# A graph kernel on one core: keys as int16 pairs for the left one-hot comparison, node numbers of the relational products in a PSUM bank, h2 transposed by fours

## The chip, the cores and the metric

One core of a Trainium2 chip runs the whole kernel as one program. The metric is the device time of an execution in microseconds (us). The engines are PE (matmuls), DVE (VectorE), ACT (ScalarE), POOL (GpSimd) and SP (which issues DMAs). SBUF is the on-chip memory; PSUM has 8 banks of 512 floats per partition.

## The reference

Two graph layers with residuals on 3125 nodes of 128 features and 50000 edges, sorted by destination, with 64 edge types. The first propagates three times over the normalized adjacency; the second is relational, with 64 relation matrices combined out of 16 bases.

```python
# layer 0
h = relu(layernorm(x));  cur = acc = h @ W_in + b_in
deg = segment_sum(1, src);  w = deg^-1/2[src] * deg^-1/2[dst]
for _ in range(3):
    cur = segment_sum(cur[dst] * w, src);  acc += cur
x = x + (acc / 4) @ W_out + b_out
# layer 1
h = relu(layernorm(x));  W_rel = einsum('rb,bio->rio', w_comp, weight)
agg = segment_sum((h @ W_rel[type])[src] * norm, dst)
x = x + relu(agg + h_bias + h @ loop_weight)
```

## The kernel before, in words

The 50000 edges lie in 391 tiles of 128, one edge per partition. The 3125 destinations are cut into 200 windows of 16 nodes, eight windows to a group of 128 nodes, 25 groups. Since the edges are sorted by destination, a step through tiles and windows has 391 + 200 - 1 = 590 pairs (tile, window). They are worked in 59 turns of U = 10 pairs.

**Setup** (to about 45 us). DVE and PE work out, for all 590 pairs at once, the destination within the window (`dlP`), the high part of the source with it (`keyP`, L649: destination times 8 plus source block) and the low part of the source (`loP`). They stand one column per pair in SBUF, as floats.

**Counting stage** (to about 345 us). It builds the dense matrix of edge counts, bf16, 128 rows per group. For each pair DVE makes two one-hot matrices over the 128 edges: the left one (128 columns, `ohA`) for five pairs in one instruction of 640 elements (L751), by comparing the numbers 0 to 127 with the pair's key, and the right one (400 columns, `ohB`, L754), one instruction per pair. There are three buffers of five pairs each. PE multiplies the two (L992) into the PSUM bank of the window; six banks go round. ACT takes two finished windows at a time out of PSUM (L1215) and clears the banks (L1217), SP writes them to their rows by DMA (L426). In turns 0 to 48, DVE, PE and POOL also make the 16 coefficients of each edge out of its type (L721, L727, L735, L1000, L518, L529); from turn 49 on PE adds the degrees in between (L1017).

**Propagation** (to about 528 us): PE's products of the dense matrix with the features (L1067), with small DVE steps between blocks, then layer norm of the result, stored to HBM as h2.

**Relational stage** (from 531 us to the end). It goes through the pairs in reverse order, from the last window to the first. POOL gathers, for each of the 391 tiles, the 128 rows of h2 of its sources from HBM by an indirect DMA whose indices lie in SBUF (L563) into a ring of 64 places (GRING); from the 65th on it waits, once for every four gathers (GSTEP), that the pairs of the tile that had the place are made. SP counts landed gathers in order for DVE. For each pair DVE copies the tile's rows next to each other (L873, 128 floats) and makes the other operand (L876, `scalar_tensor_tensor`, 256 elements): for each of 16 bases and 16 nodes of the window, coefficient if the edge's destination is that node, else zero. It compares `iota16` (int16 in SBUF) with a scalar per partition of `dlP` and multiplies by the coefficient (SBUF, float). PE multiplies (L1135, fp32, two records a pair) into one of four banks by window; ten pairs are buffered. ACT copies each closed window out (L1276) and clears its bank (L1279); after eight windows PE makes the group's output (L1115, L1116), ACT adds the bias (L1284). At the start PE transposes h2 (L1102, 25 tiles of 128) in five batches of five over two pairs of banks, 4-5 and 6-7, and ACT copies them out (L1263, 640 columns). Ahead of the last turn and behind it, outputs are transposed back into banks 6 and 7 (L1158) and added to x2 (L891).

Order: each engine's program is written out by hand; the waits on semaphores set the rest. The loop of DVE for the relational stage is a run of `operands(c)` for turns 1 to 57, then parts of `add_x2`, then turn 58.

```python
for u in range(U):                       # operands(c), L863
    if u % 2 == 0:
        dve.wait_ge(gathered, counts[u + 1][1])      # L868
        if not first:
            dve.wait_ge(pairs2, c * U + (u + 2 - U)) # L870
```

Of the kernel before, what the change touches and what calls it, by code (L numbers as in the profile page):

```python
# [34 lines left out]
I16 = mybir.dt.int16  # L35
U16 = mybir.dt.uint16
ALU = mybir.AluOpType
# [4 lines left out]
P = 128  # L42
# [4 lines left out]
BASES = 16  # L47
# [4 lines left out]
NG = -(-N // P)  # L52
# [4 lines left out]
WIN = 16  # L57
# [3 lines left out]
HI = P // WIN  # L61
LO = NPAD // HI
S = NT + NW - 1
U = 10
TURNS = S // U
HALF = S // 2
RING = 4
CRING = 6
COEF_BANK = 6
SIXTH, SIXTH_SHIFT = 10923, 16  # L70
# [10 lines left out]
HU = U // 2  # L81
# [3 lines left out]
BATCH = 5  # L85
# [6 lines left out]
H_TURNS = -(-NG // 4)  # L92
# [63 lines left out]
def build(nc, x, src, dst, etype, norm, W_in, b_in, W_out, b_out, weight, w_comp, h_bias, loop_w, out):  # L156
    assert TURNS * U == S
    ctx = ExitStack()
    with ctx:
# [15 lines left out]
        acc = sb("acc", [P, NG, HID], F32)  # L175
        stage = sb("stage", [P, WPG, LO], BF16)
        keys = sb("keys", [P, 2 * S], F32)
        keyP, loP = keys[:, 0:S], keys[:, S:2 * S]
        tab_count = sb("tab_count", [1, TURNS, len(GROUPS)], I32)
        dlP = sb("dlP", [P, S], F32)  # L180
        src_col = sb("src_col", [P, NT], I32)
        iota16 = sb("iota16", [P, LO], I16)
        ident = sb("ident", [P, P], F32)
# [27 lines left out]
        ohA = [h[:, 0:HU * P].rearrange("p (u k) -> p u k", u=HU) for h in halves]  # L211
# [6 lines left out]
        ps = ctx.enter_context(nc.psum_tensor("ps", [P, 8, 512], F32))  # L218
        psf = ps[:, :, :].rearrange("p b n -> p (b n)")
# [4 lines left out]
        at = [0]  # L224
# [14 lines left out]
        at = [0]  # L239
# [68 lines left out]
        h2T = carve2(NPAD)  # L308
# [271 lines left out]
        def _(dve):  # L580
            count = [0]

            def step(ins, wait=True):

                count[0] += 1
                ins.then_inc(dve_c, 1)
                if wait:
                    dve.wait_ge(dve_c, count[0])
# [57 lines left out]
            pairs_of = lambda b: ps[:, b:b + 2, 0:HALF]  # L646
            split = lambda row: row.rearrange("p (h s) -> p h s", h=2)
            step(dve.scalar_tensor_tensor(split(dlP[:]), split(ws_s[:]), float(-WIN), pairs_of(0), ALU.mult, ALU.add))
            step(dve.scalar_tensor_tensor(split(keyP), split(dlP[:]), float(HI), pairs_of(2), ALU.mult, ALU.add), False)  # L649
            step(dve.tensor_copy(split(loP), pairs_of(4)), False)  # L650
            step(dve.tensor_copy(src_col[:], ps[:, 6, 0:NT]), False)
            step(dve.tensor_copy(norm_col[:], ps[:, 7, 0:NT + 1]), False)
# [87 lines left out]
            def onehots(c, phase, loaded=None, stored=None, coefs=True):  # L740


                for u in range(U):
                    h = (2 * phase + u // HU) % HALVES
                    s = c * U + u
                    col = slice(s, s + 1) if isinstance(s, int) else ds(s, 1)
                    if u % HU == 0:
                        if not isinstance(s, int) or s >= HALVES * HU:
                            dve.wait_ge(pairs_done, c * U + (u - (HALVES - 1) * HU))
                        cols = slice(s, s + HU) if isinstance(s, int) else ds(s, HU)  # L750
                        dve.tensor_tensor(ohA[h][:], iota16[:, 0:P].unsqueeze(1).broadcast_to([P, HU, P]),  # L751
                                          keyP[:, cols].unsqueeze(2).broadcast_to([P, HU, P]),
                                          ALU.is_equal).then_inc(oh_ready, 1)
                    dve.tensor_scalar(ohB[h][:, u % HU, :], iota16[:], loP[:, col], None, ALU.is_equal).then_inc(oh_ready, 1)  # L754
                    if u == COEF_TYPES and loaded is not None:
                        type_rows(c, phase, loaded)
                    if u == COEF_SUM and coefs:
                        sum_parts(c - 1)
                    if u == COEF_OUT and coefs:
                        finish_coefs(c - 1, (phase - 1) % HALVES, stored)  # L760
# [91 lines left out]
            between_blocks(NB - 1)  # L852


            dve.wait_ge(ld_coef, 16)
            pairs = Turn(dve, "pair", NT)
            iota_w = iota16[:, 0:WIN].unsqueeze(1).broadcast_to([P, BASES, WIN])

            def operands(c, first=False):
                row = slice(TURNS - 1 - c, TURNS - c) if isinstance(c, int) else ds(c * -1 + (TURNS - 1), 1)  # L860
                dve.load(pairs.new_word(), tab_pair[0:1, row])
                counts = [pairs.first()]
                for u in range(U):  # L863
                    if u % 2 == 0:
# [4 lines left out]
                        if not first:  # L869
# [3 lines left out]
                    dve.tensor_copy(gpair[:, u:u + 1, :], gring[:, ds(pairs.place(total, GRING), 1), :]).then_inc(pair_in, 1)  # L873
                    dl = dlP[:, back:S - U + back + 1]
                    dl = dl[:, S - U - c * U:S - U - c * U + 1] if isinstance(c, int) else dl[:, ds(c * -U + (S - U), 1)]
                    dve.scalar_tensor_tensor(kpair[:, u, :, :], iota_w, dl,  # L876
                                             coef_flat[:, ds(tiles * -BASES + NT * BASES, BASES)].unsqueeze(2)
                                             .broadcast_to([P, BASES, WIN]),
                                             ALU.is_equal, ALU.mult).then_inc(pair_in, 1)
# [15 lines left out]
            dve.wait_ge(x2_in, 16)  # L895
            for i in range(len(OUT_PARTS) - 1):
                add_x2(i)
            operands(TURNS - 1)
            add_x2(len(OUT_PARTS) - 1)


# [1 line left out]
        def _(pe):  # L903
# [190 lines left out]
            for r in range(RING):  # L1094
                pe.matmul(ps[:, r, :], zb, zw, start=True, stop=True).then_inc(slots2, 1)
            pe.wait_ge(h2_in, 16)
            for b in range(NG // BATCH):
                if b >= 2:
                    pe.wait_ge(h2_copied, b - 1)
                for i in range(BATCH):  # L1100
                    at = 2048 + (b % 2) * 1024 + i * P
                    last = pe.transpose(psf[:, at:at + P], h2[:, b * BATCH + i, :], ident[:])  # L1102
                last.then_inc(h2_turned, 1)
            pe.wait_ge(h2_copied, NG // BATCH)
            pe.wait_ge(ld_two, 48)

            def group_output(g):
# [70 lines left out]
        def _(act):  # L1178
# [78 lines left out]
                    make_h2(b - 1)  # L1257
            make_h2(NB - 1)

            for b in range(NG // BATCH):  # L1260
                act.wait_ge(h2_turned, b + 1)
                at = 2048 + (b % 2) * 1024
                act.copy(h2T[:, b * BATCH * P:(b + 1) * BATCH * P], psf[:, at:at + BATCH * P]).then_inc(h2_copied, 1)  # L1263

            act.sem_inc(routed, 2)

# [66 lines left out]
```

## Time and profile before

| | before |
|---|---|
| median of 3 runs | 1063.05 us (1062.24 to 1063.17) |
| the profiled execution, its own time | 1060.07 us |
| its span | 1058.5 us |
| PE busy | 835.4 us (79%) |
| DVE busy | 777.0 us (73%) |
| POOL busy | 477.5 us (45%) |
| ACT busy | 357.5 us (34%) |
| mean granted TensorE clock | 0.886 of 2.4 GHz |

How to read it: busy times are sums of instructions over the whole span, so an engine that bounds one stage and rests in another shows a middling share. A duration is from an instruction's start to its end; consecutive instructions of DVE overlap by somewhat under 0.1 us, so that spacing is the better measure of cost. Releasers of waits are inferred. The spacing of POOL's instructions includes the time for issuing.

### The profile page before, as it was taken

Reading aid. Unit: us, or ns where it says so; the run is one execution under the profiler, and the core shown is the slowest. Engines: PE = TensorE matmul, PEld = TensorE weight load, DVE = VectorE, ACT = ScalarE, POOL = GpSimd, SP = SyncE. Lnnn points to the kernel's source line nnn. Section 1 sums busy time; section 2 is a strip of 40 time slices with the busy share of each in tenths; the row PEclk is TensorE's granted clock in tenths of the full one; section 3 lists DMA queues with packets and bytes.
Section 4 is the critical chain, followed back from the end, with each engine's and each line's share of the span. In section 5 each row is a group of like instructions: output and inputs, shape, how many; then the busy total and the mean of one; then the engine's idle time right before and its main releaser. Section 6 shows DMA issues by size and latency. Waiting matters only on the chain.

```text
span 1058.5 us, 27160 instructions
## 1 busy us (share of the span) xinstructions
PE 835.4 (79%) x5567; PEld 594.8 (56%) x5571; DVE 777.0 (73%) x2436; ACT 357.5 (34%) x706; POOL 477.5 (45%) x532
## 2 busy tenths in 40 slices
PE   4667667677698699999719889988888988888676
PEld 2622222222255699999517667666665665565345
DVE  7879999999984645434617777787778788888554
ACT  0402355677777000001315444443434332221000
POOL 2022323333200000010167777777777777777773
PEclk9687886977866899999858999999999999999868
DMA  4012334455534000011591111111112112111113
GB/s 114 1 45 67 85 103 107 125 131 128 132 101 107 2 1 2 1 32 51 146 298 49 48 50 50 50 50 47 52 47 52 50 50 52 50 52 51 51 50 89
DMA packets 64847, 73.24 MB, mean 69 GB/s; under 512 B 12803, under 2 KB 53178, under 8 KB 64666
## 3 DMA queue, kind: packets, MB, share of 16 engines
q1 hardware_dynamic: 48362, 37.30, 12.7%
q0 software_dynamic: 16432, 35.29, 12.6%
q8 instruction: 26, 0.43, 0.2%
q14 instruction: 27, 0.22, 0.1%
HBM read 43.85 MB, written 8.22 MB: 49 GB/s over the span
## 4 chain that ended last, share of the span: by engine, by line
PE 35%; DVE 26%; issue 15%; DVEq 9%; DMA 7%; POOL 5%; ACT 1%; SPq 1%; POOLq 0%; ACTq 0%
PE ps L1067 14%; PE ps L1135 10%; DMA CT<-h_dram,src_col 6%; POOL CT L563 5%; DVE ohbuf L754 5%; DVE CT L873 5%; PE ps L992 4%; PE ps L1115 3%; DVE u L754 3%; DVEq L876 3%; DVE CT L876 3%; DVE ohbuf L751 3%; DVEq L122 2%; DVEq L873 2%; DVE u L751 1%
## 5 line engine op out<-in xcount | busy, mean ns | idle before, releaser
L563 POOL DMA_INDIRECT CT<-h_dram,src_col x391 | 393.9, 1007 | 125.1 <-issue 95.4
L1135 PE MATMUL ps<-CT 128*128 128x256 f32 x1180 | 316.9, 418 | 71.7 <-DVE CT L876 46.3
L1135 PEld LDWEIGHTS ps<-CT 128*128 128x128 f32 x1180 | 211.3, 198 | 171.7 <-issue 151.9
L876 DVE SCALAR_TENSOR_TENSOR CT<-iota,dlP,CT 128x256 f32<-128x256 int16 x590 | 286.8, 486 | 5.6
L873 DVE COPY CT<-CT 128x128 f32 x590 | 137.7, 233 | 139.2 <-PE ps L1135 72.6
L1276 ACT COPY CT<-ps 128x256 f32<-128x256 f32 x200 | 77.7, 388 | 328.5 <-PE ps L1135 324.6
L992 PE MATMUL ps<-ohbuf 128*128 128x400 bf16 x395 | 126.6, 422 | 48.2 <-DVE ohbuf L754 34.6
L518 POOL DMA_DIRECT2D u<-types_dram x49 | 44.0, 904 | 198.8 <-PE ps L1000 185.1
L1215 ACT CAST stage<-ps 128x800 bf16<-128x800 f32 x100 | 82.4, 824 | 123.1 <-PE ps L992 122.8
L1067 PE MATMUL ps<-u,CT 128*128 128x192 bf16 x1250 | 107.4, 248 | 6.9 <-DVEq L804 6.9
L1067 PEld LDWEIGHTS ps<-u,CT 128*128 128x128 bf16 x1250 | 104.3, 99 | 9.0 <-DVEq L804 8.3
L992 PEld LDWEIGHTS ps<-ohbuf 128*128 128x128 bf16 x395 | 40.4, 102 | 122.6 <-issue 98.4
L754 DVE TENSOR_SCALAR ohbuf<-iota,keys 128x400 bf16<-128x400 int16 x395 | 102.4, 319 | 0.0
L1115 PE MATMUL ps<-CT 128*128 x800 | 95.8, 277 | 7.0 <-ACT CT L1276 4.8
L1115 PEld LDWEIGHTS ps<-CT 128*128 128x128 f32 x800 | 91.2, 191 | 16.9 <-issue 16.9
L992 PE MATMUL ps<-u 128*128 128x400 bf16 x195 | 64.3, 432 | 29.3 <-DVE u L754 17.2
L1217 ACT COPY ps<-zeros 128x800 f32<-128x800 f32 x100 | 83.0, 830 | 8.7
L551 POOL TENSOR_TENSOR ohbuf<-ohbuf,keys 128x640 f32<-128x640 f32 (+2 forms) x6 | 7.8, 1310 | 155.6 <-DMA ohbuf<-x 155.6
L1279 ACT COPY ps<-zeros 128x256 f32<-128x256 f32 x200 | 75.2, 376 | 6.5
L751 DVE TENSOR_TENSOR ohbuf<-iota,keys 128x640 bf16<-128x640 int16 x79 | 64.7, 819 | 9.5 <-PE ps L992 6.5
L1236 ACT ACTIVATE keys<-ps 128x256 f32<-128x256 f32 (+1 forms) x6 | 2.2, 366 | 161.5 <-PE ps L1041 161.5
L837 DVE COPY stage<-ps 128x320 f32<-128x320 f32 (+2 forms) x18 | 7.9, 436 | 66.2 <-PE ps L1067 65.7
(171 smaller groups left out, 653.9 us busy)
## 6 DMA issues: line engine op xcount, KB each, us to landing
CT<-stage SPq DMA_DIRECT2D x200, 100.0 KB, 3.0
u<-types_dram POOLq DMA_DIRECT2D x49, 128.0 KB, 3.5
CT<-h_dram,src_col POOLq DMA_INDIRECT x391, 2.6
coef_dram<-coef_out POOLq DMA_DIRECT2D x49, 64.0 KB, 3.4
CT<-coef_dram SPq DMA_DIRECT2D x1, 3048.0 KB, 11.9
out<-CT SPq DMA_DIRECT2D x4, 256.0 KB
ohbuf<-x SPq DMA_DIRECT2D x3, 320.0 KB, 3.8
x_dram<-ohbuf SPq DMA_DIRECT2D x3, 320.0 KB, 2.4
```

The source lines that it names most:

```text
L563: pool.indirect_dma_start(out=gring[:, (j + 1) % GRING, :], out_offset=None, in_=h2_dram, in_offset=bass.IndirectOffsetOnAxis(ap=src_col[: ...
L751: dve.tensor_tensor(ohA[h][:], iota16[:, 0:P].unsqueeze(1).broadcast_to([P, HU, P]), keyP[:, cols].unsqueeze(2).broadcast_to([P, HU, P]), ...
L754: dve.tensor_scalar(ohB[h][:, u % HU, :], iota16[:], loP[:, col], None, ALU.is_equal).then_inc(oh_ready, 1)
L873: dve.tensor_copy(gpair[:, u:u + 1, :], gring[:, ds(pairs.place(total, GRING), 1), :]).then_inc(pair_in, 1)
L876: dve.scalar_tensor_tensor(kpair[:, u, :, :], iota_w, dl, coef_flat[:, ds(tiles * -BASES + NT * BASES, BASES)].unsqueeze(2) .broadcast_to( ...
L992: pe.matmul(bank_of(count_words[at], u - lo), ohA[h][:, u % HU, :], ohB[h][:, u % HU, :], start=False, stop=True, skip_group_check=True).t ...
L1067: ins = pe.matmul(psf[:, at:at + PART], CT[:, k, m * P:(m + 1) * P], u[:, k, :], start=(k == 0), stop=(k == NG - 1))
L1115: pe.matmul(bank, wrel[:, b, :], rows, start=(b == 0), stop=False)
L1135: pe.matmul(ps[:, ds(summed.place(counts[u][0], RING), 1), 0:WIN * BASES], gpair[:, u, :], kpair[:, u, :, :].rearrange("p b d -> p (b d)") ...
L1215: act.copy(stage[:, 2 * i:2 * i + 2, :], ps[:, bank:bank + 2, 0:LO]).then_inc(staged, 1)
L1217: act.copy(ps[:, bank:bank + 2, 0:LO], zeros[:].unsqueeze(1).broadcast_to([P, 2, LO])).then_inc(slots_free, 2)
L1276: act.copy(zsb[:, half, :, j * WIN:(j + 1) * WIN], ps[:, bank, 0:WIN * BASES].rearrange("p (b d) -> p b d", b=BASES)).then_inc(zcopied, 1)
```

## The change

Three edits.

1. The keys of the left one-hot are kept as int16, each written twice side by side, in the same SBUF bytes that a float key had. The comparison L751 reads pairs from both inputs and writes pairs, so that its innermost dimension is 2 with step 1 for every operand; before, the key was one float repeated along the row. The setup step that makes the keys becomes two instructions, each of which writes 295 keys twice.
2. The 16 node numbers that L876 compares with are copied once into PSUM bank 7, as floats; all turns but the last read them there. The coefficients and the scalar stay in SBUF.
3. So that bank 7 is free, h2 is transposed in seven batches of four (the last of one), in banks 4 and 5 in turn, with ACT's copies of 512 columns.

```diff
+IOTA_BANK = 7
-        keyP, loP = keys[:, 0:S], keys[:, S:2 * S]
+        key2, loP = keys[:, 0:S].bitcast(I16), keys[:, S:2 * S]
-            step(dve.scalar_tensor_tensor(split(keyP), split(dlP[:]), float(HI), pairs_of(2), ALU.mult, ALU.add), False)
+            for h in range(2):
+                twice = lambda rows: rows.unsqueeze(2).broadcast_to([P, HALF, 2])
+                step(dve.scalar_tensor_tensor(key2[:, h * S:(h + 1) * S].rearrange("p (s e) -> p s e", e=2),
+                                              twice(dlP[:, h * HALF:(h + 1) * HALF]), float(HI),
+                                              twice(ps[:, 2 + h, 0:HALF]), ALU.mult, ALU.add), False)
-                        dve.tensor_tensor(ohA[h][:], iota16[:, 0:P].unsqueeze(1).broadcast_to([P, HU, P]),
-                                          keyP[:, cols].unsqueeze(2).broadcast_to([P, HU, P]),
-                                          ALU.is_equal).then_inc(oh_ready, 1)
+                        dve.tensor_tensor(ohA[h][:].rearrange("p u (k e) -> p u k e", e=2),
+                                          iota16[:, 0:P].rearrange("p (k e) -> p k e", e=2).unsqueeze(1)
+                                          .broadcast_to([P, HU, P // 2, 2]),
+                                          key2.rearrange("p (s e) -> p s e", e=2)[:, cols, :].unsqueeze(2)
+                                          .broadcast_to([P, HU, P // 2, 2]), ALU.is_equal).then_inc(oh_ready, 1)
+            step(dve.tensor_copy(ps[:, IOTA_BANK, 0:WIN], iota16[:, 0:WIN]))
             dve.wait_ge(ld_coef, 16)
-            def operands(c, first=False):
+            def operands(c, first=False, nodes=ps[:, IOTA_BANK, 0:WIN]):
-                    dve.scalar_tensor_tensor(kpair[:, u, :, :], iota_w, dl,
+                    dve.scalar_tensor_tensor(kpair[:, u, :, :], nodes.unsqueeze(1).broadcast_to([P, BASES, WIN]), dl,
-            operands(TURNS - 1)
+            operands(TURNS - 1, nodes=iota16[:, 0:WIN])
-            for b in range(NG // BATCH):
+            for b in range(H_TURNS):
                 if b >= 2:
                     pe.wait_ge(h2_copied, b - 1)
-                for i in range(BATCH):
-                    at = 2048 + (b % 2) * 1024 + i * P
-                    last = pe.transpose(psf[:, at:at + P], h2[:, b * BATCH + i, :], ident[:])
+                for i in range(min(4, NG - 4 * b)):
+                    last = pe.transpose(ps[:, RING + b % 2, i * P:(i + 1) * P], h2[:, 4 * b + i, :], ident[:])
-            for b in range(NG // BATCH):
+            for b in range(H_TURNS):
                 act.wait_ge(h2_turned, b + 1)
-                at = 2048 + (b % 2) * 1024
-                act.copy(h2T[:, b * BATCH * P:(b + 1) * BATCH * P], psf[:, at:at + BATCH * P]).then_inc(h2_copied, 1)
+                n = min(4, NG - 4 * b) * P
+                act.copy(h2T[:, b * 4 * P:b * 4 * P + n], ps[:, RING + b % 2, 0:n]).then_inc(h2_copied, 1)
```

## Rows read from the trace of the kernel before

**Rows 1.** Busy time per window: window, length, each engine's busy us, PEclk, DMA share, GB/s

```profile
100.00:290.00 190.00, 130.53 (x558) 52.86 (x560) 189.99 (x598) 115.58 (x141) 57.63 (x77) 0.80 0.45 115
290.00:345.00 55.00, 47.37 (x698) 27.17 (x697) 36.57 (x115) 42.00 (x52) 0.54 (x1) 0.69 0.39 103
551.00:978.00 427.00, 368.43 (x1886) 275.77 (x1885) 331.67 (x1060) 158.89 (x417) 328.25 (x325) 0.99 0.20 51
978.00:1036.00 58.00, 40.95 (x105) 25.07 (x104) 31.23 (x100) 3.06 (x8) 44.30 (x45) 0.71 0.19 50
```

**Rows 2.** Groups by line and shape, DVE, 100 to 290 us: busy us, mean ns

```profile
L754 DVE TENSOR_SCALAR ohbuf<-iota,keys 128x400 bf16<-128x400 int16 x264 | 68.9, 319 | 0.0
L751 DVE TENSOR_TENSOR ohbuf<-iota,keys 128x640 bf16<-128x640 int16 x53 | 43.4, 819 | 0.0
L751 DVE TENSOR_TENSOR u<-iota,keys 128x640 bf16<-128x640 int16 x27 | 22.0, 816 | 0.0
```

**Rows 3.** Groups by line and shape, DVE, setup steps

```profile
L666 DVE TENSOR_TENSOR CT<-CT 1x589 f32<-1x589 int16 x1 | 0.8, 764 | 0.0
L636 DVE TENSOR_TENSOR CT<-CT 128x590 int16<-128x590 int16 x1 | 0.5, 467 | 0.1
L649 DVE SCALAR_TENSOR_TENSOR keys<-dlP,ps 128x590 f32<-128x590 f32 x1 | 0.8, 770 | 0.0
```

**Rows 4.** The gathers: min/median/max ns with first and last start; two in time order; landing

```profile
L563 POOL DMA_INDIRECT CT<-h_dram,src_col x391: 940/947/1199, 531.8 to 1043.5; - x196
...
538.09 0.94 POOL L563 DMA_INDIRECT CT<-h_dram,src_col  x1 [0.30 <-issue]
548.09 0.94 POOL L563 DMA_INDIRECT CT<-h_dram,src_col  x1 [0.30 <-issue]
...
CT<-h_dram,src_col POOLq DMA_INDIRECT x391, 2.6
```

**Rows 5.** Order of time, DVE and POOL: start us, duration us

```profile
562.17 0.49 DVE L876 SCALAR_TENSOR_TENSOR CT<-iota,dlP,CT 128x256 f32<-128x256 int16 x1
562.27 1.20 POOL L563 DMA_INDIRECT CT<-h_dram,src_col  x1 [0.30 <-issue]
```

**Rows 6.** Groups by line, DVE and ACT from 551 us, POOL from 531 us, to 792 us

```profile
L876 DVE SCALAR_TENSOR_TENSOR CT<-iota,dlP,CT 128x256 f32<-128x256 int16 x290 | 140.7, 485 | 2.7
L1276 ACT COPY CT<-ps 128x256 f32<-128x256 f32 x128 | 49.7, 388 | 125.3 <-PE ps L1135 121.5 <-issue 1.0
L563 POOL DMA_INDIRECT CT<-h_dram,src_col x196 | 201.0, 1025 | 65.7 <-issue 49.4 <-DVE CT L873 9.1 <-DMA h_dram<-ohbuf 6.3
```

**Rows 7.** Order of time, turns of the relational stage on PE and DVE

```profile
943.60 5.03 PE L1135 MATMUL ps<-CT 128*128 128x256 f32 x20 [1.50 <-DVE CT L873]
...
970.52 0.23 DVE L873 COPY CT<-CT 128x128 f32 x1 [0.78 <-PE ps L1135]
...
976.96 0.48 DVE L876 SCALAR_TENSOR_TENSOR CT<-iota,dlP,CT 128x256 f32<-128x256 int16 x1
978.22 0.23 DVE L873 COPY CT<-CT 128x128 f32 x1 [0.78 <-PE ps L1135]
...
1034.30 0.48 DVE L876 SCALAR_TENSOR_TENSOR CT<-iota,dlP,CT 128x256 f32<-128x256 int16 x1
...
1041.78 0.23 DVE L873 COPY CT<-CT 128x128 f32 x1 [0.29 <-issue]
```

**Rows 8.** Groups by line and shape, DVE, two-source steps of the propagation

```profile
L841 DVE TENSOR_TENSOR stage<-stage,dis 128x320 f32<-128x320 f32 x9 | 4.4, 491 | 1.3
L838 DVE TENSOR_TENSOR stage<-ps,stage 128x320 f32<-128x320 f32 x9 | 4.4, 491 | 0.3
```

**Rows 9.** Groups by line and shape, ACT, copies of transposed tiles

```profile
L1187 ACT COPY CT<-ps 128x512 f32<-128x512 f32 x6 | 3.5, 579 | 4.8 <-PE ps L942 4.8
L1263 ACT COPY CT<-ps 128x640 f32<-128x640 f32 x5 | 3.4, 694 | 22.0 <-PE ps L1102 22.0
```

More of the change, by code:

```diff
@@ L852, in _ @@
             between_blocks(NB - 1)
+            step(dve.tensor_copy(ps[:, IOTA_BANK, 0:WIN], iota16[:, 0:WIN]))
             dve.wait_ge(ld_coef, 16)
             pairs = Turn(dve, "pair", NT)
-            iota_w = iota16[:, 0:WIN].unsqueeze(1).broadcast_to([P, BASES, WIN])
-            def operands(c, first=False):
+            def operands(c, first=False, nodes=ps[:, IOTA_BANK, 0:WIN]):
                 row = slice(TURNS - 1 - c, TURNS - c) if isinstance(c, int) else ds(c * -1 + (TURNS - 1), 1)
@@ L1096, in _ @@
             pe.wait_ge(h2_in, 16)
-            for b in range(NG // BATCH):
+            for b in range(H_TURNS):
                 if b >= 2:
                     pe.wait_ge(h2_copied, b - 1)
-                for i in range(BATCH):
-                    at = 2048 + (b % 2) * 1024 + i * P
-                    last = pe.transpose(psf[:, at:at + P], h2[:, b * BATCH + i, :], ident[:])
+                for i in range(min(4, NG - 4 * b)):
+                    last = pe.transpose(ps[:, RING + b % 2, i * P:(i + 1) * P], h2[:, 4 * b + i, :], ident[:])
                 last.then_inc(h2_turned, 1)
-            pe.wait_ge(h2_copied, NG // BATCH)
+            pe.wait_ge(h2_copied, H_TURNS)
             pe.wait_ge(ld_two, 48)
```

## The prediction

> **What bounds the kernel now.** I cut the span into stretches by the busy time per window [rows 1], then read each stretch that the diff touches by groups of lines and in order of time. "Same" below means within 0.2% of the time before, about what a measurement of this kernel can tell from no change.
>
> The counting stage, 100 to 290 us: DVE is busy 189.99 of 190 us, PE 130.5, ACT 115.6 [rows 1]. DVE alone sets the pace. There are 80 instructions of L751 in it, two to a turn [rows 2], so a turn takes 190/40 = 4.75 us, and the two comparisons of L751 (819 and 816 ns) are its largest single items. From 290 to 345 us the turns carry no coefficients but PE has the degree sums: PE is busy 47.4 of 55 us, ACT 42.0, DVE 36.6. That stretch is PE's and ACT's.
>
> The relational stage, 551 us to the end: three engines are close. The reader is to see first that POOL is saturated: 325 gathers in 427 us. Left alone it starts one every 1.25 us (eight from 538.09 to 548.09), but over the stage it needs (1043.5 - 531.8)/390 = 1.31 us, because many instructions take up to 1199 ns in place of 940 [rows 4]. A long one begins inside L876: the gather at 562.27 takes 1.20 us, and L876 had started at 562.17 with 0.49 us to run [rows 5]. The largest lengthening, 1199 - 940 = 259 ns, is what 256 elements of L876 take at 1.04 ns each. So L876 holds the gather up.
> Does the gather set the time? For most of the stage it does not. At 792 us DVE has made 290 pairs and ACT has closed 128 windows, so about 290 - 128 = 162 tiles are in use, while 196 gathers have been issued [rows 6]: 34 tiles ahead. Later windows hold many tiles, so that nearly each pair costs a gather, and DVE catches up. By 978 us it has made 530 pairs (the window's 1060 instructions are 530 copies and 530 products). A turn had taken 978.22 - 970.52 = 7.70 us until then; with 6.44 us from the first copy to the last product of a turn (976.96 - 970.52), the next four take (1034.30 - 978.22 - 6.44)/4 = 12.4 us each [rows 7]. In that stretch POOL, with 45 gathers in 58 us, is what ends last.
>
> **The change part by part.**
>
> *Keys in int16 pairs (L751).* The comparison reads int16 node numbers and keys as adjacent int16 twins and writes bf16: all 2-byte. Its new duration is bounded above by 819 ns (nothing gained) and below by the rate of L754, 400 elements in 319 ns with one source, which at a quarter cycle for each of 240 more is some 380 ns [rows 2]. The nearest row is a two-source operation with int16 in and out, L636: 590 elements in 467 ns, against 764 ns for 589 of L666 with a float result [rows 3], 0.504 ns an element less. I take that, since sources and widths are the same: 640 x 0.504 = 323 ns saved, 819 to 496. In turns 0 to 48 DVE is the bound: 98 x 0.323 = 31.7 us, less 0.7 for turn 1, in which DVE may wait for PE's first products: **-31.0 us**. The twenty comparisons of turns 49 to 58 (6.5 us) I cost at nothing, since PE's 47.4 of 55 us cover them; as DVE comes to them further ahead, PE may wait less, 0 to 3 us more. What is late next: a counting turn would be 4.75 - 0.65 = 4.10 us. ACT needs 115.6/40 = 2.9 us of it; PE 130.5/40 = 3.3 at a mean granted clock of 0.80, more where it is at the lower level (1.2 GHz). Up to 5 us could be lost there, kept for the range.
>
> *Making the keys (L649).* One instruction of 590 elements (770 ns, [rows 3]) becomes two of 590; DVE's setup is on the path: **+0.7 us**.
>
> *Node numbers in PSUM (L876).* This takes away one of two SBUF inputs. What a PSUM input does to the duration is seen in L838 (PSUM and SBUF) against L841 (both SBUF): 491 and 491 ns for 320 elements [rows 8]. I take no change of its 485 ns. The bounds: 60 ns less (in first products of a turn POOL may be the one that holds DVE) and 267 ns more (a pass at half rate; no row re-reads a short PSUM row sixteen times).
> The Trainium skill speaks against this move: VectorE: DVE Perf Modes, section "The TRN2 errata", gives a fixed 120 cycles to an operation from PSUM, 58 to one from SBUF. By that the product would be 62 cycles, an estimated 65 ns, longer. The trace disagrees with it at L838 and L841.
> The gather: if what held it was DVE's second read from SBUF, its period becomes 1.25 us and the last one starts at 531.8 + 390 x 1.25 = 1019.3 in place of 1043.5. The Trainium skill has this rule (SBUF — State Buffer, section "Who interferes with whom"): a Vector instruction with two SBUF inputs contends with a GpSimd instruction that reads SBUF. By that rule, the trace agrees, and one input fewer ends it.
> How much of the 24 us reaches the end? Up to 978 us nothing, since DVE and PE set that pace: ten products of PE take 5.03 us behind 1.50 us of idle time [rows 7], plus the groups' outputs. After 978 us the turns stay at DVE's 7.70: turn 57 starts at 978.22 + 4 x 7.70 = 1009.0, its last product at 1015.5 in place of 1034.30: **-18.8 us**. Gathers keep up: the last lands by 1019.3 + 0.94 + 2.6 (the time to landing, [rows 4]) = 1022.8, and the last turn starts at 1041.78 - 18.8 = 1023.0. The ring doesn't fill: at 792 us there are (792 - 531.8)/1.25 = 208 gathers, 46 ahead of 162, and there are 64 places, freed in fours. The bounds of this term: 0 (the hold-up stays) to 22 (2 to 3 us more from first products).
> The copy into bank 7 before the stage (16 columns, some 0.2 us with its wait) lies in the time before 551 us in which DVE waits for the first gathers and the coefficients; without that cover it costs 0.2 us. The last turn reads SBUF as before, since transposes have bank 7 by then.
>
> *h2 by fours.* PE still makes 25 transposes; ACT makes six copies of 512 (579 ns) and one of 128 in place of five of 640 (694 ns) [rows 9], 3.8 for 3.5 us, which run beside PE's transposes. I cost it at nothing; uncovered it is 0.4 us.
>
> The sum: 1060.1 (the profiled execution; its span is 1058.5) - 31.0 + 0.7 - 18.8 = 1011. The median of the runs is 3.0 above the profiled one; a part of that goes on top: **1012 us**. Own range of this case: 1004 (3 from the last counting turns, 2 from first products, some from PE and ACT waiting less) to 1021 (5 lost to PE's clock, a fifth of the 18.8 lost).
>
> **The rivals.**
> 1. *The gather stays held*, because L876 still reads its coefficients, and L873 its rows, from SBUF. For: both stay. Against: the 259 ns fit a whole pass of L876, too long for the 128 elements of L873, and L876 is to keep but one input. Then the last turns stay at 12.4 us: 1060.1 - 31.0 + 0.7 + 1.5 = 1031. Chance 0.09.
> 2. *A PSUM input costs a fixed 65 ns*, as a mechanism: no DVE turn under 8.35 us. In order of time 34 of the first 53 turns take 7.7 to 7.8 us; lifted to 8.35 they add about 22 us, and the last product of turn 57 comes at 978.2 + 22 + 4 x 8.35 + 7.0 = 1040.6, 6 us later than before: 1060.1 - 31.0 + 0.7 + 6 + 1.5 = 1037. Rows 8 speak against. Chance 0.07. The skill's errata rule gives this case.
> 3. *The pairs don't double the rate*, because the key operand repeats one pair 64 times, which L636 does not; the change then doesn't do what it says: 1060.1 + 0.7 - 18.8 = 1042. For: no row repeats a pair. Against: the old form repeats one key 128 times at full rate. Chance 0.06.
> 4. *Slower than before:* L876 re-reads a 64-byte PSUM row sixteen times; if that runs at half rate, each product is 267 ns longer: 57 turns of 7.70 + 2.67 = 10.37 us plus 9.1 are 600 us, where it was 1034.3 - 551.0 = 483: +117, and 1060.1 - 30.3 + 117 = 1147 us. It decides from about 120 ns a product, where turns of 8.9 us use up what the keys gave. For: no such read is in the trace. Against: the same pattern on SBUF runs at full rate (L876 itself). Chance 0.03.
>
> **How the numbers follow.** The forecast has 0.75. The range, 1004 to 1036, takes in its own range and rival 1; left out are rivals 2 to 4 (0.16) and a little of the forecast's edges. All but rival 4 are far below 1063; 0.02 goes to costs of several parts together that cancel the gain: faster 0.95, same 0.02, slower 0.03.
>
> **What would show each step.** L751 near 0.50 us, counting turns near 4.1 us with DVE still busy in all of them, the propagation starting some 30 us earlier. L876 at 485 ns, gathers at 940 to 950 ns, 1.25 us apart. Turns at 7.7 us to the end, with DVE no longer waiting for gathers. It would be wrong if L876 grew by more than 20 ns, if gathers of 1.1 us stayed, if counting turns took 4.3 us or more, or if the ring filled.

## The result and the profile after

The changed kernel takes 1011.79 us, the median of four runs (1010.13 to 1014.49), against 1062.64 us (1060.84 to 1063.17) for the kernel before on the same chip: a ratio of 0.9527, with a 95% interval of 0.9502 to 0.9551. The forecast was 1012. The profiled execution took 1010.13 us with a span of 1008.6 (before: 1060.07 and 1058.5).

The busy time per window of the changed kernel, with the columns of [rows 1]: counting with coefficients, counting with degree sums, and the relational stage in two parts.

```profile
100.00:260.00 160.00, 112.70 (x533) 46.66 (x533) 159.02 (x580) 111.86 (x137) 45.98 (x75) 0.94 0.53 131
260.00:315.00 55.00, 47.02 (x700) 27.43 (x700) 29.59 (x108) 43.02 (x54) 0.54 (x1) 0.72 0.42 108
520.00:940.00 420.00, 363.36 (x1863) 271.70 (x1862) 324.10 (x1043) 157.87 (x416) 317.60 (x337) 0.99 0.21 55
940.00:990.00 50.00, 37.71 (x148) 24.74 (x146) 39.39 (x122) 3.83 (x10) 37.81 (x41) 0.97 0.20 53
```

DVE is still busy all through the counting (159.02 of 160 us), so what the comparison saves shortens every turn. PE's granted clock there is 0.94 where it was 0.80 [rows 1]. The last line is what [rows 1] showed as PE 41 of 58 us with POOL late; now PE is busy 37.7 of 50 us at 0.97.

The groups of DVE by line and shape, 100 to 260 us; the comparison of keys is L756 now (L751 before), the right one-hot L761 (L754), the scaling of coefficients L740:

```profile
L761 DVE TENSOR_SCALAR ohbuf<-iota,keys 128x400 bf16<-128x400 int16 x257 | 66.6, 316 | 0.0
L761 DVE TENSOR_SCALAR u<-iota,keys 128x400 bf16<-128x400 int16 x130 | 33.6, 314 | 0.0
L756 DVE TENSOR_TENSOR ohbuf<-iota,keys 128x640 bf16<-128x640 int16 x51 | 24.6, 483 | 0.2 <-PE ps L999 0.2
L756 DVE TENSOR_TENSOR u<-iota,keys 128x640 bf16<-128x640 int16 x26 | 12.5, 482 | 0.4
L740 DVE TENSOR_TENSOR coef_out<-coef_sum,norm_col 128x128 f32<-128x128 f32 x39 | 10.9, 280 | 0.0
```

The comparison took 819 and 816 ns in [rows 2] and takes 483 now. The groups of the page for the relational stage, with the gathers (L564), the products (L883) and the copies of rows (L880):

```profile
L564 POOL DMA_INDIRECT CT<-h_dram,src_col x391 | 369.8, 946 | 125.2 <-issue 97.2
...
L883 DVE SCALAR_TENSOR_TENSOR CT<-ps,dlP,CT 128x256 f32<-128x256 f32 x580 | 279.4, 482 | 4.5
L880 DVE COPY CT<-CT 128x128 f32 x590 | 146.9, 249 | 121.7 <-PE ps L1141 62.6
```

A gather now takes 946 ns in the mean, no more than 1011, where [rows 4] had up to 1199 (1007 in the mean). The product did not grow: 482 ns against 485 in [rows 6]. In order of time, at the two ends of the relational stage, first the kernel before (first pair, start of turn 57), then the changed one (copy of the node numbers, first gather, first pair, start of turn 57, last gather, first pair of the last turn, its products on PE):

```profile
550.98 0.23 DVE L873 COPY CT<-CT 128x128 f32 x1 [23.14 <-SPq L480]
...
1023.20 0.23 DVE L873 COPY CT<-CT 128x128 f32 x1 [1.30 <-SPq L480]
```

```profile
497.96 0.18 DVE L862 CAST ps<-iota 128x16 f32<-128x16 int16 x1
...
501.78 1.01 POOL L564 DMA_INDIRECT CT<-h_dram,src_col  x1 [6.31 <-DMA h_dram<-ohbuf]
...
519.49 0.23 DVE L880 COPY CT<-CT 128x128 f32 x1 [21.36 <-SPq L481]
...
977.45 0.23 DVE L880 COPY CT<-CT 128x128 f32 x1 [0.79 <-SPq L481]
...
989.45 0.94 POOL L564 DMA_INDIRECT CT<-h_dram,src_col  x1 [0.30 <-issue]
...
990.74 0.23 DVE L880 COPY CT<-CT 128x128 f32 x1 [0.29 <-issue]
...
992.16 7.38 PE L1141 MATMUL ps<-CT 128*128 128x256 f32 x20 [2.38 <-DVE CT L883]
```

Where the 49.9 us of the spans came from, with [rows 4, 7] for the other starts of before:

| stretch | before | after | difference |
|---|---|---|---|
| to the first gather | 531.76 | 501.78 | -29.98 |
| first gather to first pair | 19.22 | 17.71 | -1.51 |
| first pair to turn 57 | 472.22 | 457.96 | -14.26 |
| turn 57 to the last turn | 18.58 | 13.29 | -5.29 |
| last turn to the end | 16.72 | 17.86 | +1.14 |

The starts of every tenth copy give the turns. Turns 1 to 52 have the same lengths in both kernels within 0.14 us (7.71, 8.34, 9.5, 10.2 us and so on, in the same order). Turns 53 to 57 took 8.39, 11.78, 12.38, 12.43 and 18.58 us before, and take 7.72, 7.71, 7.71, 7.70 and 13.29 now.

### The profile page after: what moved, and what is told of

Read it like the earlier page. It is cut to its first block, busy times and chain, and to the rows that moved or that the text cites. A ratio compares the mean times of both kernels' runs of the same rounds, so it can differ in the third digit from the quotient of the medians.

```text
span 1008.6 us, 27165 instructions
## 1 busy us (share of the span) xinstructions
PE 805.6 (80%) x5567; PEld 581.8 (58%) x5571; DVE 737.5 (73%) x2438; ACT 357.0 (35%) x708; POOL 443.6 (44%) x532
## 4 chain that ended last, share of the span: by engine, by line
PE 37%; DVE 23%; issue 14%; DVEq 9%; POOL 8%; DMA 6%; SPq 2%; ACT 1%; POOLq 0%; ACTq 0%
PE ps L1074 14%; PE ps L1141 12%; POOL CT L564 8%; PE ps L999 5%; DMA CT<-h_dram,src_col 5%; DVE ohbuf L761 5%; DVE CT L880 4%; DVE CT L883 2%; DVE u L761 2%; DVEq L883 2%; PE ps L1121 2%; DVEq L123 2%; DVE coef_sum L732 2%; DVEq L880 1%; DVE ohbuf L756 1%
## 5 line engine op out<-in xcount | busy, mean ns | idle before, releaser
L564 POOL DMA_INDIRECT CT<-h_dram,src_col x391 | 369.8, 946 | 125.2 <-issue 97.2
L1141 PE MATMUL ps<-CT 128*128 128x256 f32 x1180 | 306.0, 408 | 64.2 <-DVE CT L880 32.9
L1141 PEld LDWEIGHTS ps<-CT 128*128 128x128 f32 x1180 | 205.9, 193 | 158.9 <-issue 140.3
L883 DVE SCALAR_TENSOR_TENSOR CT<-ps,dlP,CT 128x256 f32<-128x256 f32 x580 | 279.4, 482 | 4.5
L880 DVE COPY CT<-CT 128x128 f32 x590 | 146.9, 249 | 121.7 <-PE ps L1141 62.6
L999 PE MATMUL ps<-ohbuf 128*128 128x400 bf16 x395 | 119.1, 384 | 35.7 <-DVE ohbuf L761 14.1
L519 POOL DMA_DIRECT2D u<-types_dram x49 | 32.7, 672 | 181.1 <-PE ps L1007 167.1
L761 DVE TENSOR_SCALAR ohbuf<-iota,keys 128x400 bf16<-128x400 int16 x395 | 101.6, 316 | 0.0
L1121 PEld LDWEIGHTS ps<-CT 128*128 128x128 f32 x800 | 91.2, 191 | 16.8 <-issue 16.8
L999 PE MATMUL ps<-u 128*128 128x400 bf16 x195 | 57.2, 362 | 28.6 <-DVE ohbuf L761 16.9
L999 PEld LDWEIGHTS ps<-u 128*128 128x128 bf16 x195 | 18.8, 96 | 60.6 <-issue 50.4
```

The lines of the kernel that those rows point to most:

```text
L564: pool.indirect_dma_start(out=gring[:, (j + 1) % GRING, :], out_offset=None, in_=h2_dram, in_offset=bass.IndirectOffsetOnAxis(ap=src_col[: ...
L883: dve.scalar_tensor_tensor(kpair[:, u, :, :], nodes.unsqueeze(1).broadcast_to([P, BASES, WIN]), dl, coef_flat[:, ds(tiles * -BASES + NT * ...
L999: pe.matmul(bank_of(count_words[at], u - lo), ohA[h][:, u % HU, :], ohB[h][:, u % HU, :], start=False, stop=True, skip_group_check=True).t ...
L1121: pe.matmul(bank, wrel[:, b, :], rows, start=(b == 0), stop=False)
L1141: pe.matmul(ps[:, ds(summed.place(counts[u][0], RING), 1), 0:WIN * BASES], gpair[:, u, :], kpair[:, u, :, :].rearrange("p b d -> p (b d)") ...
```

## The experiments

Three series, each beside runs of the kernel before on its own chip: 1059.4 us there for the first four kernels, 1060.55 for the next four, 1060.61 and 1059.01 for the last two. Ratios are to these. The changed kernel's 1011.79 us stands beside 1062.64 for the kernel before, so a difference from it in microseconds is uncertain by some 3 us between chips, and the ratio is the safer measure. Line numbers shift by a few between the kernels.

### Each part alone

**e1_keys_only**: the kernel before with the int16 pairs (setup and comparison), nothing else of the change.

> The kernel before with the int16 key pairs alone. Theory (the two gains lie one behind the other): the comparison at 485 ns, the first gather some 30 us earlier than before, gathers as before with a mean near 1007 ns, last turns of 12.4 us: 30 to 31 us below before, ratio 0.971. Rival (the gains overlap, since the new node numbers also helped through an earlier start): under 27 us.

Measured: 1031.81 us (1031.49 to 1032.58), ratio 0.9739 (0.9721 to 0.9757), 27.6 us less where 30 to 31 were expected. The comparison takes 484 ns, the first gather starts at 503.18, 28.6 us sooner than before (29.98 in the changed kernel, whose setup and counting are the same, so that the difference is scatter), and the gathers are held as before:

```profile
L564 POOL DMA_INDIRECT CT<-h_dram,src_col x391 | 394.2, 1008 | 125.6 <-issue 95.4 <-DVE CT L880 17.7 <-DMA h_dram<-ohbuf 6.7
L883 DVE SCALAR_TENSOR_TENSOR CT<-iota,dlP,CT 128x256 f32<-128x256 int16 x590 | 286.4, 485 | 5.5
```

**e2_psum_only**: the kernel before with the node numbers in bank 7 and h2 by fours; float keys, read once.

> The kernel before with the node numbers in PSUM and h2 by fours, keys as floats. Theory (DVE's second SBUF read held the gathers): gathers at 940 to 950 ns, turns 53 to 57 at 7.7 us in place of 12.4, 19 to 20 us below before, ratio 0.982. Rival (it is only the sum that works, POOL being met earlier by the keys' gain): near 0 to 10 us.

Measured: 1039.63 us (1038.79 to 1040.58), ratio 0.9811 (0.9793 to 0.983). Turns stay at 7.7 us to the end. The lead, the number of gathers issued beyond the tiles in use, grows to 50; the ring has 64 places.

```profile
L564 POOL DMA_INDIRECT CT<-h_dram,src_col x391 | 369.5, 945 | 125.1 <-issue 96.9 <-DVE CT L874 14.3 <-DVE CT L877 7.6
L877 DVE SCALAR_TENSOR_TENSOR CT<-ps,dlP,CT 128x256 f32<-128x256 f32 x580 | 279.2, 481 | 4.5
```

**e3_fours_only**: the kernel before with the seven batches of h2's transposes, as in the diff, and nothing else.

> The kernel before with h2 transposed by fours alone. Theory (PE's transposes and DVE's wait for the gathers hide ACT's copies): within 1 us of before, first pair at the same distance from the first gather (19.2 us). Rival (the earlier first copy lets the relational stage begin sooner, which the 1.5 us found there come from): 1 to 1.5 us below.

Measured: 1060.26 us over ten runs (1058.1 to 1062.46), ratio 1.0004 (0.9993 to 1.0016): nothing. From the first gather to the first pair it is 19.2 us, as before, so the 1.5 us that the changed kernel saves there do not come from this edit.

The spans of the profiled executions (1030.1 and 1038.0 against 1058.5) give 28.4 and 20.5 us, 48.9 together; the whole change gives 49.9. The two parts add up, since each lies in its own stage.

### Why the gathers run free

**e4_float_nodes_sbuf**: the changed kernel, but the sixteen node numbers stand as floats in SBUF.

```diff
-            step(dve.tensor_copy(ps[:, IOTA_BANK, 0:WIN], iota16[:, 0:WIN]))
+            step(dve.tensor_copy(nodes_f[:], iota16[:, 0:WIN]))
-            def operands(c, first=False, nodes=ps[:, IOTA_BANK, 0:WIN]):
+            def operands(c, first=False, nodes=nodes_f[:]):
```

> The changed kernel with the 16 node numbers as floats in SBUF, not in PSUM. Theory (what held the gathers is that both inputs are read from SBUF, whatever their type): gathers up to 1200 ns and a mean near 1005, last turns of 12.4 us, 18 to 20 us slower than the changed kernel. Rival (the int16 type with its conversion was the cause): gathers stay at 945 ns and the time is that of the changed kernel within 1 us.

Measured: 1032.28 us (1029.59 to 1032.76), ratio 0.9743 (0.9726 to 0.9761): all that the second part gives is gone, with the type as in PSUM. Its gathers last up to 1222 ns and 1005 in the mean, the last one begins at 1012.08.

```profile
L565 POOL DMA_INDIRECT CT<-h_dram,src_col x391 | 392.9, 1005 | 125.2 <-issue 95.4 <-DVE CT L881 18.9 <-DMA h_dram<-ohbuf 6.3
L884 DVE SCALAR_TENSOR_TENSOR CT<-nodes_f,dlP,CT 128x256 f32<-128x256 f32 x590 | 286.3, 485 | 5.8
...
1012.08 1.22 POOL L565 DMA_INDIRECT CT<-h_dram,src_col  x1 [0.30 <-issue]
```

What frees the gather is that one of the product's two inputs leaves SBUF. The Trainium skill (SBUF — State Buffer, section "Who interferes with whom") states that a Vector instruction with two SBUF inputs contends with a GpSimd instruction that reads SBUF; this pair of kernels agrees.

The trace of the kernel before shows how long a gather is held. Those that begin 100 to 150 ns behind the start of a product last 232 ns longer than 940 in the mean, those at 200 to 250 ns 135 longer, those at 250 to 300 ns 93. Those that begin 350 ns or more behind it last at most 7 ns longer, and of the 36 that begin less than 100 ns behind it only two are held, at 98 and 99 ns. So a gather that begins inside this stretch of the product waits until some 360 ns of the product are over, and then takes its usual time.

### Why the comparison is faster

**e5_int16_single**: the changed kernel; the key is an int16, read once per row with step 0 innermost.

```diff
-                                          key2.rearrange("p (s e) -> p s e", e=2)[:, cols, :].unsqueeze(2)
-                                          .broadcast_to([P, HU, P // 2, 2]), ALU.is_equal).then_inc(oh_ready, 1)
+                                          key2.rearrange("p (s e) -> p s e", e=2)[:, cols, 0:1].broadcast_to([P, HU, P]),
+                                          ALU.is_equal).then_inc(oh_ready, 1)
```

> The changed kernel, but the comparison reads each int16 key once and repeats it along the row (innermost step 0 on the key) instead of reading twins. All operands stay 2-byte. Theory (two results a cycle need adjacent pairs in every operand): the comparison is back at 817 ns and the time 29 to 31 us above the changed kernel, near 1041. Rival (2-byte types alone do it, the twins are idle): 485 ns and the time of the changed kernel within 1 us.

Measured: 1041.74 us (1039.51 to 1042.07), ratio 0.9818 (0.9799 to 0.9837).

```profile
L756 DVE TENSOR_TENSOR ohbuf<-iota,keys 128x640 bf16<-128x640 int16 x79 | 64.5, 816 | 9.3 <-PE ps L997 9.1
```

816 ns, as with float keys: the narrow type alone gives nothing. The key has to be there twice, next to itself.

### How deep the ring must be

**e6_ring32**: the changed kernel with `GRING = 32` for 64.

> The changed kernel with a ring of 32 places for gathered tiles in place of 64. Theory (the gathers' lead, 49 tiles at its peak, is used up in the last turns, and a lead of some 30 would run out): POOL is held in the middle, some 19 gathers x 1.25 us = 24 us are missing at the end, of which some 3 are slack: 19 to 21 us slower than the changed kernel. Rival (DVE and PE set the pace to the end, the lead is no matter): within 3 us.

Measured: 1036.36 us (1035.9 to 1037.44), ratio 0.9774 (0.9757 to 0.9792), 24.6 us more than the changed kernel; by ratio it is 26. I had expected 19 to 21. In the profiled executions the first gather starts 2.4 us later (504.14 against 501.78), where the edit does nothing. Single gathers are as short as before, but POOL waits for places: its idle time is 153.6 us where it was 125.2.

```profile
L564 POOL DMA_INDIRECT CT<-h_dram,src_col x391 | 369.9, 946 | 153.6 <-issue 95.1 <-DVE CT L883 26.8 <-DVE CT L880 25.2
...
1020.17 0.94 POOL L564 DMA_INDIRECT CT<-h_dram,src_col  x1 [0.30 <-issue]
```

The lead stops at 29 tiles and is down to 3 or 4 from turn 53 on, and the turns of the end take 10 to 12 us again. The gain of the second part is thus a stock: free gathers build up 49 tiles (38 before) while DVE and PE set the pace, and the end, where each pair costs a new tile, lives on it. With room for 32 most of it is lost though each gather is as fast.

### Is the counting stage still DVE's?

**e7_product_on_pool**: the changed kernel; the scaling of coefficients (L740, 280 ns on DVE, 39 in 160 us) goes to POOL, which was busy 46 of these 160 us.

> The changed kernel with the product of coefficients and edge weights (280 ns on DVE, one per counting turn) made by POOL. Theory (DVE alone bounds the counting turns, 4.08 us each): 49 x 0.22 = 11 us at most, of which the last ten or so turns give little since ACT is near its bound there: 6 to 10 us below the changed kernel. Rival (POOL's reads of SBUF and DVE's two-input and 2-port instructions hold each other up, or ACT and PE bound the turns): 0 to 4 us below, or slower.

Measured: 1011.64 us (1009.93 to 1012.93), ratio 0.9542 (0.9527 to 0.9557): no gain, the rival's case; 6 to 10 us had been forecast. DVE's groups and its window, 100 to 260 us:

```profile
L770 DVE TENSOR_SCALAR ohbuf<-iota,keys 128x400 bf16<-128x400 int16 x256 | 72.4, 337 | 0.0
L770 DVE TENSOR_SCALAR u<-iota,keys 128x400 bf16<-128x400 int16 x129 | 35.2, 329 | 0.0
```

```profile
100.00:260.00 160.00, 111.74 (x534) 46.19 (x535) 158.60 (x538) 111.99 (x137) 62.73 (x115) 0.95 0.52 132
```

42 instructions fewer (538 for 580), yet DVE is as busy. The right one-hots, 385 here and 387 there, take 107.6 us in place of 100.2, which eats 7.4 of the 10.9 us that left. In the whole run 53 of the 590 last over 400 ns, up to 741, and each of the 53 overlaps a multiplication on POOL; the changed kernel has one over 400 ns. The other 3.5 us don't show in time either, and what took them wasn't tried. The Trainium skill (SBUF — State Buffer, section "Who interferes with whom") states that `tensor_scalar` in its fastest modes uses the ports it shares with GpSimd and is then blocked by it, or blocks it. The longer L770 agree; that the ports are their cause was not tried apart. Turns 0 to 47 are as long as in the changed kernel (206.16 us for 206.19 in all): handing this product to POOL bought DVE nothing.

### What holds the end now

**e8_no_row_copy**: the changed kernel without the copy L880. The gathered rows are not moved, so PE multiplies by whatever the buffer holds; that part of the computation is left out.

> The changed kernel without the copy of gathered rows in front of each relational product (the products use old rows; that part of the output is left out), which takes about 0.25 us per pair from DVE. Theory (after the change POOL's unbroken gathers are again the floor, only about a microsecond under DVE): the last gather starts no earlier than in the changed kernel, and the time is 0 to 3 us below it. Rival (DVE is the one bound of the stage): turns of 5.2 to 6.5 us where PE allows, 10 us or more below.

Measured: 1006.15 us (1005.85 to 1006.45), ratio 0.9487 (0.9471 to 0.9503). With some 150 us of DVE's work gone it is only 5.6 us less (5.5 less than e7 on the same chip), more than the 3 us at most that I had given it and far from what a DVE-bound stage would give.

Two things hold it. First, most of the stage is not DVE's: from 520 to 940 us PE is busy 364.5 us, as with the copies (363.4), though DVE is busy 229.6 for 324.1. Turns of 6.5 and of 9.5 us alternate, and turn 57 starts 7.1 us sooner, at 970.35; which waits give the 9.5 us was not followed. Second, at the end the gathers come last. Its end in order of time (start of the last turn, last gather, the wait of the last pairs, their products on PE), and SP's last counts of landed gathers:

```profile
986.93 2.54 DVE L882 SCALAR_TENSOR_TENSOR CT<-iota,dlP,CT 128x256 f32<-128x256 int16 x6 [0.25 <-issue]
...
989.47 0.94 POOL L564 DMA_INDIRECT CT<-h_dram,src_col  x1 [0.30 <-issue]
...
993.61 0.88 DVE L882 SCALAR_TENSOR_TENSOR CT<-iota,dlP,CT 128x256 f32<-128x256 int16 x2 [3.09 <-PE ps L1140]
994.73 1.13 PE L1140 MATMUL ps<-CT 128*128 128x256 f32 x4 [1.13 <-DVE CT L882]
...
L484 SPq EVENT_SEMAPHORE  x6: 17/17/17, 985.7 to 993.4; - x6
```

The last gather starts at 989.47, as in the changed kernel (989.45), and the last pair waits until 993.61. The wait is put down to PE, which had nothing to give; what came last is SP's count of the last gather, at 993.4. That is 4.0 us after this gather began, where the three before it and the changed kernel's last one were counted 2.5 us after their starts; why this one landed some 1.5 us late is open, and it makes this time longer than the floor alone would. The floor itself is POOL's: 501.8 + 390 x 1.25 = 989.3 for the start of the last gather, as long as a gather takes 1.25 us, and it moves with the first gather.

### A faster version: the order of the loads

A part of the 17.7 us from the first gather to the first pair could still be had, up to that floor. SP issues the load of the coefficients (3 MB), of h2 (1.6 MB) and of x2 (1.6 MB, needed only before the last turn) around the first gather, and is held 10.05 us by the last issue.

**e9_x2_later**: the changed kernel, x2 loaded after the 192nd gather.

> The changed kernel (1011.8 us), with SP's load of x2 (3125 rows, 1.6 MB, needed only ahead of the last turn) issued after the 192nd gather is counted rather than before the first. Its issue held SP for 10.05 us of the 17.7 us between the first gather (501.78) and the first pair (519.49), and DMAs were busy all that time at 290 to 415 GB/s. Theory (the first pair waits for gathers that share the DMA engines with this load, and the counted turns behind it keep their lengths until POOL's gathers stop them): the first pair comes 3 to 5 us sooner, turns keep their 458 us, the last gather still starts at 987 to 990 us, the last turn starts near 987 and its last pair waits for the last gather, as where the copies were left out: 1006 to 1008.5 us, 3 to 5 us less than the changed kernel. Rival A (the 3 MB of coefficients and h2 alone hold the first gathers): first pair moved by under 1 us, 1011 to 1012 us. Rival B (x2's load disturbs the gathers in the middle as much): first pair earlier, but a few turns near the 192nd gather longer, 1010 to 1013 us.

Measured: 1011.77 us (1009.93 to 1012.89), ratio 0.9536 (0.951 to 0.9562): no gain. The first pair does come 10 us sooner, but PE has to transpose h2 before its first product, and h2 comes no sooner (517.13, against 516.65 in the changed kernel):

```profile
509.32 0.23 DVE L885 COPY CT<-CT 128x128 f32 x1 [11.60 <-SPq L478]
...
517.13 3.38 PE L1113 MATMUL ps<-ident,CT 128*128 128x128 f32 x16 [18.43 <-DMA CT<-h_dram]
...
526.00 0.23 DVE L885 COPY CT<-CT 128x128 f32 x1 [10.99 <-SPq L478]
```

The third line is the start of turn 1: 526.00, against 526.66. None of the three cases that I had written down was this one; I had moved one of two waits that end close together.

**e10_h2_first**: as e9, and h2 is loaded ahead of the coefficients.

```diff
-            sp.dma_start(coef[:, 0:NT - U, :].rearrange("p t b -> p (t b)"),
-                         coef_dram[:, 0:(NT - U) * BASES]).then_inc(ld_coefs, 16)
...
             sp.dma_start(h2[:], h2_dram.rearrange("(g p) f -> p g f", p=P)).then_inc(h2_in, 16)
+            sp.dma_start(coef[:, 0:NT - U, :].rearrange("p t b -> p (t b)"),
+                         coef_dram[:, 0:(NT - U) * BASES]).then_inc(ld_coefs, 16)
```

> The changed kernel (1011.8 us) with SP's loads at the start of the relational stage in another order: h2 (1.6 MB) first, the coefficients of turns 1 to 58 (3 MB) behind it, x2 (1.6 MB) after the 192nd gather. With x2 alone moved, DVE had its first pair at 509.3 in place of 519.5, but PE still waited for h2 until 517.1, and turn 1 began at 526.0. Theory (PE's wait for h2 is what ends last, then, at the other end, POOL's last gather): PE's transposes start at 507 to 510, turn 0 and PE's first products follow by 515, turn 1 waits for the coefficients at 515 to 518 (6.2 less 1.6 MB at 300 to 400 GB/s), turns keep their lengths, and the last pair waits for the last gather, whose start stays at 989 to 990: last turn starts by 987, 1005 to 1007.5 us, 4 to 7 us less than the changed kernel, no more, as where the copies were left out (1006.15). Rival A (something else holds PE, or the coefficients now come as late as h2 did): turn 1 at 523 or later, 1009 to 1012 us. Rival B (no floor by the last gather: the last turn moves as far as the first one): turn 1 and the last turn both 9 us earlier, 1001 to 1003 us.

Measured: 1006.79 us (1006.47 to 1008.15), ratio 0.9506 (0.9493 to 0.952). Every run of it is below every run of the changed kernel, and it computes all of the reference. How much it gains is less sure, since the chips differ: 5.0 us by the medians, 3.3 by the profiled spans, 2 to 3 by the ratios (0.9527 for the changed kernel, 0.9536 for e9), whose intervals overlap.

```profile
509.75 5.25 PE L1113 MATMUL ps<-ident,CT 128*128 128x128 f32 x25 [11.02 <-DMA CT<-h_dram]
512.59 0.27 DVE L885 COPY CT<-CT 128x128 f32 x1 [14.84 <-SPq L478]
...
520.52 0.23 DVE L885 COPY CT<-CT 128x128 f32 x1 [2.22 <-PE ps L1146]
...
974.60 0.23 DVE L885 COPY CT<-CT 128x128 f32 x1 [1.22 <-PE ps L1146]
...
977.06 0.23 DVE L885 COPY CT<-CT 128x128 f32 x1 [1.20 <-PE ps L1146]
...
988.30 0.23 DVE L885 COPY CT<-CT 128x128 f32 x1 [0.29 <-SPq L489]
...
989.25 1.04 POOL L569 DMA_INDIRECT CT<-h_dram,src_col  x1 [0.30 <-issue]
```

PE's transposes start 6.9 us sooner, turn 1 6.1 us (520.52 for 526.66) and turn 57 7.0 us (970.41, by the starts of the copies). The last turn starts only 2.4 us sooner, 988.30, since the lead of gathers is down to 4 tiles at turn 57 and the last of them still starts at 989.25: the floor again, but one turn earlier than I had written. From its third pair on turn 57 makes two pairs in some 2.45 us (974.60 to 977.06), the time of two gathers, where the changed kernel takes 1.4. The last pair doesn't wait for the last gather: it starts at 994.02, and SP counts that gather at 991.9. The span is 1005.3 us.

## Why the prediction was right, point by point

The mechanisms held in both parts. That the forecast of 1012 us met the median within 0.2 us is luck: the four runs spread over 4.4 us, and the profiled spans differ by 49.9 us for a sum of 49.1 while terms of up to 1.5 us on both sides of it partly cancel.

- **Keys in pairs, -31.0 us.** The per-instruction estimate was a little cautious (496 ns expected, 483 measured); the turn was right. Turns 0 to 47 are 0.647 us shorter each ((282.39 - 45.15)/48 before, (251.54 - 45.35)/48 after, from the starts of turns 0 and 48), where the prediction had 0.65. That is 31.1 us, and it repeats: in all twelve traces these turns take 236.3 to 237.3 us with a comparison of 0.82 us and 206.2 to 206.6 with one of 0.48. L636, an int16 step of 590 elements [rows 3], was a good neighbour for a comparison with a bf16 result. Rival 3, that a repeated pair doesn't double the rate, is out; e5 shows what it would have been, 816 ns and 1042 us, the number given for it.
- **Making the keys, +0.7.** The two instructions take 767 ns each, and the start of turn 0 moved by 0.20 us, which does not measure the term: turn 0 starts at 44.68 to 45.15 us in the three traces with the one-instruction setup and at 44.99 to 46.44 in the nine with two, 0.6 us apart in the mean. Behind turn 48 the changed kernel gives 0.9 us back (10 turns 45.62 for 45.35 us, propagation 204.62 for 204.02), where the own range had 0 to 3 us more gain; why is open. So the first gather moved by 29.98 where the sum had 30.3. That closeness is partly luck: the first gather starts at 530.26 to 531.76 us in the four traces with the slow comparison and at 501.25 to 504.14 in the eight with the fast one, 28.5 us apart in the mean.
- **PE's clock.** I kept up to 5 us for a loss as PE falls behind. The opposite happened: granted 0.94 for 0.80 in this stage. PE is busy 70% of it now (112.7 of 160), 69% before (130.5 of 190).
- **The product reads PSUM at no cost.** 482 ns for 485; rivals 2 and 4 (+65 and +267 ns a product) are out. The rule of the Trainium skill weighed there (VectorE: DVE Perf Modes, section "The TRN2 errata") is not borne out by this product either: no 62 cycles are added.
- **The gathers, -18.8 us.** Right in kind and in size: mean 1.25 us apart, (989.45 - 501.78)/390. Turns are 7.71 to the end, and to the start of the last turn the stage is 14.26 + 5.29 = 19.6 us shorter, against 18.8. Two readings under this term were off and did no harm. The four turns behind 978.22 did not take 12.4 us each: turn 57 starts at 1023.20, so turns 53 to 56 took 8.39 to 12.43 us, 11.2 in the mean, and the rest lay in turn 57 itself, whose products spread over 11.1 us for the 6.44 assumed. The sum ended at the last product of turn 57, for which only the total counts; it starts 464.4 us behind the first pair now and 483.3 before, 18.9 less. And the time to landing runs from a gather's start, so 0.94 us was counted twice: the changed kernel's last gather starts at 989.45 and SP counts it at 992.0. Rival 1 is out, and e4 shows its world at 1032 (1031 was given). The peak of the lead was put at 46 tiles by a reading at 792 us; it is 49.
- **What was not in the sum.** 1.5 us fewer between the first gather and the first pair (the issue of x2's load holds SP 10.05 us for 11.58; e3 rules out the transposes; it is 16.4 to 18.5 us in traces with the fast comparison and the same order of loads, 18.9 to 19.2 with the slow one, and stays open), and 1.1 us more at the very end: PE's last 20 records take 7.38 us in place of 6.28, at a granted clock of 0.61 for 0.76 in their windows. The two nearly cancel. First products of a turn gave nothing; the range had kept up to 3 us for them.
- **h2 by fours, 0**, and the copy to bank 7, hidden (497.96, 0.18 us, 21 us before the first pair): right, e3 and the timeline.

The sum of the spans' differences is 49.9 us, and the forecast's -31.0 + 0.7 - 18.8 was 49.1.

## What to carry to other kernels

The two-input comparison of 16-bit data on DVE took 483 ns for 816 only with its broadcast key stored twice, side by side; the narrow type alone gave nothing, and the second copy costs one more setup instruction. When POOL issues gathers beside DVE, look at the spread of the gather's duration: if its longest exceeds its shortest by about a pass of a two-input DVE instruction (259 to 282 ns here, for 256 elements), try one small input in PSUM. A faster producer pays only where there is room to stock its lead, and once it is the floor (here 390 x 1.25 us from the first gather), cuts in the consumer's work, even 150 us of them, return only what is left above it, and no more than the other engines of the stage let through.

## What the runs showed of the hardware that was not expected

- DVE's copies of rows grew as its products let the gathers go: 249 ns in the mean with the node numbers in PSUM (e2 and the changed kernel), 233 and 234 with two SBUF inputs (e4, e1). In the changed kernel 77 of the 590 take over 300 ns, up to 473; in the kernel before it was 14, up to 444. Part of the conflict thus changed sides, from POOL to a DVE that has slack there; no turn grew by it. Which access does it was not tried.
- A gather issued on POOL while DVE's two-input product was between 100 and 350 ns old was held until some 360 ns; one issued later was not (the kernel before).
- A multiplication on POOL lengthened 400-element DVE comparisons beside it, to 741 ns at worst (e7).
- One issue on SP's queue can hold SP for 8.8 to 12.1 us while the DMA engines are full (share 0.95 from 502.3 to 512.3 us in the changed kernel), and with it the counting of gathers that DVE waits for; the same load issued later, at 743 us, held it 0.72 us (e9). Ordering three loads by first use was worth 2 to 5 us (e10).
